# One program block instead of six, a routing pipeline in quarter-batch units, folded linear attention and a routed stage three tiles deep

## What is computed

```python
x = x + 0.5 * ffn(layernorm(x))
x = x + attn(layernorm(x))
x = x + 0.5 * ffn(layernorm(x))

# ffn: 16 experts in 4 groups, top 2 groups, top 2 experts; plus a shared expert
scores = softmax(xf @ gate_w.T); orig = scores; scores = scores + gate_b
...                                          # keep the 2 best groups, then the 2 best experts
h  = silu(xf @ We1[e] + be1[e]) * (xf @ We3[e] + be3[e])      # 256 -> 128
y  = sum over the 2 chosen e of weight[e] * (h @ We2[e] + be2[e])
z  = (silu(xf @ ws1 + bs1) * (xf @ ws3 + bs3)) @ ws2 + bs2     # shared: 256 -> 256 -> 256

# attn: 16 heads of 16, relu feature map, no softmax
q, k, v = split(x @ w_qkv.T);  q = relu(q);  k = relu(k)
z = 1 / (ksum . q + eps);  out = (context @ q) * z,  context = v k^T per head
attn = out @ w_proj.T + b_proj
```

## Time and profile before

| | us |
|---|---|
| median of 3 runs | 1683.13 |
| lowest, highest | 1672.27, 1699.55 |
| profiled execution, its own time | 1687.54 |
| its span, first to last instruction | 1685.8 |

### The profile page before, as it was taken

How to read it: one execution, slowest core, us unless ns; L and a number is a source line. 1 busy time by engine, 2 the same in 40 slices (tenths; PEclk the granted TensorE clock), 3 DMA queues, 4 the chain that set the end, 5 groups by cost and what they waited for, 6 DMA issues and landing times. The chain is left out here.

```text
span 1685.8 us, 29173 instructions
## 1 busy us (share of the span) xinstructions
PE 1338.1 (79%) x7304; PEld 973.1 (58%) x7304; DVE 847.4 (50%) x3339; ACT 680.1 (40%) x1488; POOL 608.3 (36%) x732
## 2 busy tenths in 40 slices
PE   4888788599878882999999987888877699998910
PEld 3545455377767772666666654555444488887800
DVE  1655544456555554244444433544555366666645
ACT  2323332066555552443333323332332176666600
POOL 1444455545444442000000001455554455554510
PEclk9989999799999996999999996999999699999955
DMA  5911111444434332111111000111111555444368
GB/s 195 300 54 51 51 63 68 124 134 143 121 120 118 118 110 102 51 50 50 50 50 50 0 1 1 51 61 63 61 64 57 131 159 148 146 146 120 119 244 353
DMA packets 83451, 172.84 MB, mean 103 GB/s; under 512 B 16856, under 2 KB 59885, under 8 KB 76915
## 3 DMA queue, kind: packets, MB, share of 16 engines
q1 hardware_dynamic: 54902, 93.25, 18.4%
...
## 5 line engine op out<-in xcount | busy, mean ns | idle before, releaser
L976 POOL DMA_INDIRECT routed_rows<-xn,rdest x288 | 281.8, 979 | 307.7 <-DVE rw L965 188.3
L887 PE MATMUL bank<-rows 128*128 128x128 f32 x2304 | 313.2, 280 | 9.6 <-ACT rows L919 6.5
L887 PEld LDWEIGHTS bank<-rows 128*128 128x128 f32 x2304 | 283.9, 194 | 20.2 <-ACT rows L919 17.3
L450 PE MATMUL bank<-xnT,ws 128*128 128x512 f32 x512 | 264.2, 646 | 38.8 <-DVE work L591 19.9
L805 POOL DMA_INDIRECT expert_rows<-rows,slots x256 | 248.7, 971 | 101.1 <-issue 76.8
L898 PE MATMUL bank<-w,rows 128*128 x576 | 178.5, 392 | 50.7 <-DVE rows L946 50.1
L946 DVE SCALAR_TENSOR_TENSOR rows<-bank,tile_b,rows 128x128 f32<-128x128 f32 x288 | 101.0, 351 | 225.4 <-ACT rows L924 178.6
L468 PE MATMUL bank<-ws,work 128*128 128x256 f32 x512 | 149.5, 425 | 51.5 <-DVE work L591 35.4
L919 ACT COPY rows<-w 128x512 f32 x288 | 178.2, 619 | 14.6 <-issue 8.3
L450 PEld LDWEIGHTS bank<-xnT,ws 128*128 128x128 f32 x512 | 94.8, 204 | 129.2 <-issue 99.9
L916 ACT COPY rows<-bank 128x256 f32<-128x256 f32 x288 | 106.5, 370 | 148.2 <-PE bank L877 135.6
...
## 6 DMA issues: line engine op xcount, KB each, us to landing
...
```

The costliest lines, as they stand in the source:

```text
L450: last = nc.tensor.matmul(bank[:], ws[:, c, mi * P:(mi + 1) * P], m.xnT[:, c, g * HALF:(g + 1) * HALF], start=c == 0, stop=c == KC - 1)
L887: last = nc.tensor.matmul(h_ps[t.slot(2)][:, n * P:(n + 1) * P], m.rw13[:, t.slot(2), c * C + n * INTER:c * C + (n + 1) * INTER], m.rT[:, ...
L976: nc.gpsimd.indirect_dma_start(out=d.yt, out_offset=bass.IndirectOffsetOnAxis(ap=m.rdest[:, y.slot(SLOTS):y.slot(SLOTS) + 1], axis=0), in_ ...
```

## The change

The kernel is rewritten as one block. No barrier stands between the stages any more, all loops over batches are written out with constant semaphore counts, and each engine runs its whole program from setup to store.

- **Route.** The shared expert is cut into quarters of a batch: per quarter two `up` units (4 matmuls of 256 columns; h1 and h3 share one bank, 4 banks in turn) and one `down` unit (2 tiles), 99 units a layer. `FIRST` and `TAIL` assign the units to batches. Around them each engine puts its part of the routing: PE the gate matmuls of batch b (one tile after each matmul) and the transposes of batch b+1 (one group of 4 at `SPOTS`), DVE three to five steps of `route_work` after each unit's `gated` or `add_shared`. `xs` and `xnT` have three buffers; the places of batch b are made and its rows are scattered while batch b+1 is computed. The routing data are written into the rows by ACT (`meta`) rather than POOL, and POOL keeps one of its four statistics steps (the power).
- **HELD.** The last 9 slots of units of each layer (4 ups, 3 downs, 2 empty) are computed behind the routed stage, not ahead of it.
- **Routed stage.** Three buffers (`RB`) for the transposes, weights, silu, gated and output banks. PE's step holds the transposes of tile i+2, up of i, down of i-2.
- **Attention.** v is not computed for every token. PE makes the 256 x 256 matrix G = xn^T k over the tokens (`gram`), then context = w_v G, masked to the heads, then M = context x w_proj (`mixer`), so the output is relu(q) z times M in one matmul a tile. The denominators are made on DVE from q and the key sums (`sum_keys`, `scale`), which PE spreads over the partitions (`spread_ksum`). Routed rows come in pieces of 512 KB in 3 buffers; the last attention batch also does the normalisation and transposes of layer 1's first batch.
- **Final.** 16 pieces of 1 MB in 6 buffers, stores of 512 KB.

```diff
-        setup_stage(nc, m, d, sem)
-        ffn_route_stage(nc, m, d, sem, 0)
-        routed_stage(nc, m, d, sem, 0)
-        attention_stage(nc, m, d, sem)
-        ffn_route_stage(nc, m, d, sem, 1)
-        routed_stage(nc, m, d, sem, 1)
-        final_stage(nc, m, d, sem)
+        program(nc, m, d, sem)
...
+YSLOTS = 3
+RB = 3
+XS = 3
+PIECES = 2
+FSLOTS = 6
...
+UNITS = 3 * (ALL_Q + 1)
+FIRST = (0, 10, 19, 29, 38, 47, 57, 66, 75)
+TAIL = range(75, 90)
+HELD = range(90, UNITS)
+SPOTS = (3, 4, 6, 7)
+RANK_AT, TABLES_AT, BIASES_AT = 0, 6, 9
...
+def unit_of(n):
+
+    q, k = divmod(n, 3)
+    if k < 2:
+        return (q, "up", k) if q < ALL_Q else None
+    return (q - 1, "down", 0) if q else None
...
+            def up(L, q, mi, between):
...
+                pe.wait_ge(s.xT_copied, 4 * r + 2 * (part // 2) + 2)
+                wait(pe, s.gated_ready, u - 3)
...
+            def down(L, q, between):
+                n = L * ALL_Q + q
+                pe.wait_ge(s.gated_ready, 2 * n + 2)
+                wait(pe, s.y_added, n - 1)
...
+                    for k, n in enumerate(range(FIRST[b], FIRST[b + 1])):
+                        if more and k in SPOTS:
+                            transpose(r + 1, SPOTS.index(k))
+                        shared(L, n, gate_next)
+                        if b and k == RANK_AT:
+                            rank(r - 1)
+                for k, n in enumerate(TAIL):
+                    shared(L, n)
...
+                for i in range(-2, TILES + 2):
+                    t = L * TILES + i
+                    if routed(i + 2):
...
+                        last.then_inc(s.rT_ready, 1)
+                    if routed(i):
+                        pe.wait_ge(s.rw13_copied, t + 1)
+                        pe.wait_ge(s.rT_copied, t + 1)
+                        wait(pe, s.rgated_ready, t + 1 - RB)
...
+                    if routed(i - 2):
+                        y = t - 2
+                        e = expert_at(i - 2)
+                        pe.wait_ge(s.rgated_ready, y + 1)
...
+            for b in range(BATCHES):
+                more = b + 1 < BATCHES
+                for i in range(NT):
+                    gram(b, i)
+                    if i + 2 < NT:
+                        keys(b, i + 2)
+                queries(b, 0)
+                spread_ksum(b)
+                queries(b, 1)
+                context(b)
+                queries(b, 2)
+                queries(b, 3)
+                mixer(b)
+                for p in range(PAIRS):
+                    transpose_q(b, p)
+                    if p:
+                        outputs(b, p - 1)
+                    if more:
+                        a_transpose(b + 1, p)
+                    else:
+                        transpose(BATCHES, p)
...
+                    for k, n in enumerate(range(FIRST[b], FIRST[b + 1])):
+                        shared(L, n)
+                        for _ in range(((0 if b else 3), 4, 5, 3)[min(k, 3)]):
+                            next(work, None)
```

1894 lines of the change are left out of this document (975 added, 919 removed).

## The result

Time after: 1556.45 us, median of 6 runs (1553.11 to 1562.59), against 1695.49 for the kernel before in the same comparison (six runs, 1672.27 to 1724.78). The ratio is 0.9258, 95% interval 0.9197 to 0.9318: faster by 7%, where 1400 was predicted, with a range that ended at 1490. The ratio is of the means without the kernel before's three slowest runs, which lie over 1.5% above its fastest (the two medians would give 0.918). The profiled execution took 1554.16 us, its span 1552.1.

What follows compares the result with a forecast made beforehand. PE's work bounds attention and the second routed stage, waits the route and first routed stages. From 1685.8 us, gains of 148 (route), 75 (routed), 36 (attention) and 28 (ends) gave 1400 us, range 1325 to 1490.

Steps and rivals of the forecast that it cites:

- Late signals thus keep a quarter of what they cost now: Route stages: PE's late signals cost little with more slack, so a batch takes 31 us instead of 37.6.
- 0 to 7 us late, say 3: Route stages: assumed lateness of PE's signal to silu, part of a 5.3 us loop before each down.
- so little shows: End of route stages: the last batch's scatters run under the 15 tail units, 28 us, and so hardly add time.
- a lead of 5.7 us: Route stages: PE work between a down's second up and the down itself; 0.6 us charged for each of four downs.
- charged 0.3 us: Route stages: added wait for each group of transposes, which needs ACT's copy of the one before and has 1.8 us.
- so a signal that is 2 us late no longer stops PE: Routed stages: two steps, 3.3 us, from up to down instead of one; 247 us each, for 301.9 and 266.5.
- The 6 us for a slow clock in the first batch: Layer 0's route stage: 6 us added because PE starts almost idle, with a granted clock near 0.5.
- HELD was given 27 us: Route stages: 13.4 us of units taken off each and moved behind the routed stage, while the last rows land.
- A: Rival, whole kernel: four banks and two-step slack absorb every late signal; 1347 us, chance 0.17.
- B: Rival: late signals come back; batches at 36 us, tiles at 1.77, 4 us attention hole; 1516 us, chance 0.2.
- C: Rival, route stages: each unit pays its own late signal, 3.85 us; 75 us a batch, 2100 in all, chance 0.05.
- D: Rival, between stages: queues still drain without barriers, so the gaps stay (28 us); 1428 us, chance 0.08.

Runs made afterwards that it cites:

- On time: Kernel before, unaltered, run again on an occasion when none of PE's signals came late: 1557.50 us.
- on-time 1406: Changed kernel, unaltered, run again on an occasion when none of PE's signals came late: 1406.54 us, ratio 0.9027 to the kernel before.

## Why the prediction was wrong

**The step that failed** is "Late signals thus keep a quarter of what they cost now". They cost 35 and 37 us in the route stages, where the forecast charged 2.3 us a batch, 18 a stage, and where the kernel before had paid 24 and 26. What was missed is the length of the hold at three places. I took "0 to 7 us late, say 3" for every stretch alike, and batches 2 to 5 indeed pay nothing for lateness. But the change's pipeline leaves three unbroken runs of scatters at the end of each layer, two of them under batch 8 and the 15 tail units, of which I wrote "so little shows": 22 us did. The wait that was longest, 7.89, is moreover not one for a down, to which I gave a lead of 5.7 us, but for a group of transposes, to which I gave 1.8 and charged 0.3 us: 11.4 us of lateness met a lead of 4.1. The granted clock is lower after it, and further holds follow.

**The second one** is "so a signal that is 2 us late no longer stops PE", worth 75 us of the 287. A signal 2 us late does not, the lead is 2.43; but with three buffers it came 3.6 us late. I held the lateness fixed while changing what makes it. The gain measured is 17.8 in layer 0 and -14.5 in layer 1.

**My reading of before** laid all of 37.6 - 28.7 = 8.9 us of a route batch to lateness. On time a batch of that kernel takes 33.8 (98.4 to 132.2 and to 166.0), so 3.8 were lateness; the other 5.1 I lay to the coarse order of its units and routing steps, which no run changes by itself. The forecast also has too little for what stops the new loop apart from late signals. Batches 2 to 5 take 27.8 us each, late and on time, with 37 units between them; by the forecast they would take 4 x 31 less the 11 units that come later at 1.9 us, 25.8 each, and without its charge for late signals 23.5. PE's waits for ACT's copies (16.1 us in the stage) and for the first rows (6.5) make up most of the 25 us for which it is not busy in the on-time route stage. The transposes were charged 0.3 us a group, 1.2 a batch, and even this is not in the 31.1. The 6 us for a slow clock in the first batch did not come: the granted clock was 1.00 from 21.8 to 52.1, as it had been in the first batch before (26.80 to 58.50 in the earlier trace rows).

So it is luck that the forecast of 1400 is near the on-time 1406. The forecast was for late signals, and what it charged for them, 18 us a stage, is near what the on-time stages pay for something else.

**Right:** attention, 37.7 us in one batch for 36.9, with 26.4 us of DVE for 24:

```profile
658.70:696.40 37.70, 35.39 (x184) 30.32 (x184) 26.39 (x55) 15.02 (x32) 1.64 (x1) 1.00 0.19 57
```

Also the gap, the vanished join and the end, each within 4 us. HELD was given 27 us and is worth 7. The rule of the Trainium skill (page "SBUF — State Buffer", section "Who interferes with whom") that a DVE instruction with two SBUF inputs and a GpSimd one that reads SBUF shut each other out stays without support: scatters stand 1.27 us apart (203.35 to 222.37 in 15 steps), as before, and no further apart up to 214.8, amid DVE's routing steps, than behind. Whether a scatter counts as such a reading instruction no run here shows. Of the rivals, A (1347) is beaten by the on-time 1406 already. B named the right thing, late signals that come back. Its 80 us for the route stages came out (75), though not spread evenly as it had them; its tiles at 1.77 us gave 20 where 71 came, and its hole in attention, 16, did not come (6), so with 1516 it fell 40 us short. C did not occur: its 3.85 us for each unit would need a hold in each unit. Nor did D: start, gap and end are 5.0, 1.6 and 5.2 us shorter, and the join of 16.9 is gone.
